# Batch 0's hi/lo parts stored to DRAM by halves of the heads, the first group's rows read between the two halves' stores

## The reference

```python
qkv = x @ w_qkv
q, k, v = jnp.split(qkv, 3, axis=2)                    # each (8, 512, 128) -> (8, 16, 512, 8)
att = jnp.einsum('bhtd,bhsd->bhts', q, k) / np.sqrt(D)
att = jnp.where(causal, att, -jnp.inf)
out = jnp.einsum('bhts,bhsd->bhtd', softmax(att), v)
x = layernorm(x + out.transpose(0, 2, 1, 3).reshape(B, T, C))
gate, up = x @ (w_gate/127).T, x @ (w_up/127).T
x = layernorm(x + (silu(gate) * up) @ (w_down/127).T)
```

## Time and profile before

| | us |
|---|---|
| three runs | 361.03, 364.29, 364.29 (median 364.29) |
| the profiled execution | 362.71 |
| its span, first to last instruction | 361.0 |
| TensorE busy | 338.2 (94%) |
| VectorE busy | 291.8 (81%) |
| ScalarE busy | 214.6 (59%) |
| GpSimd busy | 180.2 (50%) |

### The profile page before, as it was taken

One profiled execution on the slowest core, in us unless ns is written; L12 is line 12 of the kernel. 1 busy time (PEld: TensorE's weight loads), 2 busy tenths in 40 slices (PEclk: granted clock), 3 DMA queues, 4 the chain that ended last, 5 costly groups with the idle time before them and its releaser, 6 DMA issues.

```text
span 361.0 us, 9029 instructions
## 1 busy us (share of the span) xinstructions
PE 338.2 (94%) x2907; PEld 198.4 (55%) x2911; DVE 291.8 (81%) x1247; ACT 214.6 (59%) x277; POOL 180.2 (50%) x329
## 2 busy tenths in 40 slices
PE   4878999999999999999999999999999998999971
PEld 2533445556455645655564556556445544898961
DVE  6875658898888888988988898899898884868653
ACT  2400447877777677777867676876677774434310
POOL 8400133653384455447335734653433578787552
PEclk9996559999999999999999999999999969999997
DMA  4798330276337426532661553166200010011111
GB/s 145 279 301 246 83 86 5 63 254 190 91 126 229 120 63 236 155 112 86 228 190 37 188 170 120 33 237 202 66 4 5 5 30 3 1 36 53 46 44 58
DMA packets 33902, 41.73 MB, mean 116 GB/s; under 512 B 3136, under 2 KB 17472, under 8 KB 33856
## 3 DMA queue, kind: packets, MB, share of 16 engines
q1 hardware_dynamic: 33856, 41.17, 36.0%
HBM read 21.76 MB, written 18.87 MB: 113 GB/s over the span
## 4 chain that ended last, share of the span: by engine, by line
PE 79%; DVE 9%; issue 5%; DMA 3%; ACT 2%; POOL 1%; SPq 0%; DVEq 0%; POOLq 0%; ACTq 0%
PE psum L500 21%; PE psum L477 18%; PE psum L460 14%; PE psum L681 5%; DVE masked L853 5%; PE psum L416 5%; PE psum L407 4%; PE psum L669 3%; PE psum L671 3%; PE psum L442 2%; PE psum L509 2%; PE psum L432 2%; DMA scr_k<-parts 1%; DVE nm L853 1%; DMA xa<-L_attn_x 1%
## 5 line engine op out<-in xcount | busy, mean ns | idle before, releaser
L853 DVE CUSTOM_DVE_ANT_0 masked<-psum,mask 128x384 bf16<-128x384 f32 (+3 forms) x512 | 219.2, 487 | 37.5 <-PE psum L477 30.6
L756 ACT ACTIVATE pt<-psum 128x1024 f32<-128x1024 f32 x160 | 158.4, 1021 | 59.7 <-PE psum L460 59.2
L1028 POOL TENSOR_SCALAR_AFFINE_SELECT pt<-pt 128x512 f32<-128x512 f32 x128 | 79.7, 635 | 101.5 <-ACT pt L756 99.5
L477 PE MATMUL psum<-kx,qx 33*128 33x384 f32 (+3 forms) x512 | 93.5, 366 | 3.3 <-DMA kx<-scr_k 1.8
L500 PE MATMUL psum<-pt,vx 128*32 128x256 f32 (+2 forms) x1280 | 94.8, 397 | 0.1
L460 PE MATMUL psum<-qx,kx 35*128 35x384 f32 (+3 forms) x512 | 77.7, 353 | 0.9 <-DMA qx<-nm_T 0.8
L477 PEld LDWEIGHTS psum<-kx,qx 33*128 33x128 f32 x512 | 54.3, 193 | 40.9 <-DVE nm L853 19.1
L460 PEld LDWEIGHTS psum<-qx,kx 35*128 35x128 f32 x512 | 47.2, 192 | 30.4 <-issue 16.1
L500 PEld LDWEIGHTS psum<-pt,vx 128*32 128x32 f32 x1280 | 30.7, 110 | 39.0 <-issue 26.0
L853 DVE DVE_READ_ACCUMULATOR2_ANT nm<- 128x1 f32 x512 | 42.5, 83 | 0.0
L1016 POOL TENSOR_SCALAR nm_parts<-nm 128x16 fp32r<-128x16 f32 x32 | 6.6, 207 | 51.4 <-DVE nm L853 50.3
(11 more groups left out here) (64 smaller groups left out, 268.6 us busy)
## 6 DMA issues: line engine op xcount, KB each, us to landing
scr_q<-parts SPq DMA_DIRECT2D x16, 512.0 KB, 3.7
scr_k<-parts SPq DMA_DIRECT2D x16, 512.0 KB, 5.5
qx<-scr_q SPq DMA_DIRECT2D x64, 128.0 KB, 2.6
kx<-scr_k SPq DMA_DIRECT2D x64, 128.0 KB, 2.7
xa<-L_attn_x SPq DMA_DIRECT2D x8, 256.0 KB, 3.3
res<-L_attn_x SPq DMA_DIRECT2D x8, 256.0 KB, 2.8
out<-yo SPq DMA_DIRECT2D x8, 256.0 KB, 2.3
qx<-nm_T SPq DMA_DIRECT2D x64, 8.0 KB
```

The source lines that it names most:

```text
L477: last = pe.matmul(bank[:, col:col + width], qx[u][at:at + KM, 2 * g + hh // 2, P * i:P * i + P].bitcast(F32R), kx[u][at:at + KM, 2 * g + ...
L756: act.activation(pt[G % 2][:, 2 * s:2 * s + 2, :], pair_of("S", G, s), ACT.Exp, scale=SM_SCALE).then_inc(exp_done, 1)
L853: dve.tensor_tensor_reduce(masked[count % 4][:, 0:width], bank[:, col:col + width], mask[:, T - width:T], -1.0, 3.0e38, ALU.add, ALU.min, ...
L1028: pool.affine_select(out=blocks, in_=blocks, pattern=[[0, HG], [1, P]], compare_op=ALU.is_ge, fill=0.0, base=0, channel_multiplier=-1).the ...
```

## The change

Only batch 0 is touched. `write_half(half)` stores the 64 partitions of one half of the heads, again four DMAs, now of 256 KB each, with a semaphore of its own for each half. SP issues the first half's four stores, reads group 0's rows, issues the second half's four stores, and then reads the rows of groups 1, 2 and 3. A read of batch 0 waits for its own half alone. The later batches' stores are as they were, and their waits count from one batch less. `parts_of_1` on VectorE waits for both halves.

```diff
+        scr_half = [sem(f"scr_half{half}") for half in range(2)]
...
+            def write_half(half):
+
+                at = slice(64 * half, 64 * half + 64)
+                for n, scr in enumerate((scr_q[0], scr_k[0])):
+                    for part, made in enumerate((hi_made, lo_made)):
+                        sp.wait_ge(made, n + 1)
+                        terms = (scr[at, 2 * part:2 * part + 2, :], scr[at, part::2, :])[n]
+                        sp.dma_start(terms, parts[at, n, part, :].unsqueeze(1).to_broadcast([64, 2, T])).then_inc(scr_half[half], 16)
+
             def read_rows(b, u, g):
                 half, par = g // 2, g % 2
-                sp.wait_ge(scr_written, SCR * b + SCR)
+                if b == 0:
+                    sp.wait_ge(scr_half[half], SCR)
+                else:
+                    sp.wait_ge(scr_written, SCR * b)
...
-            write_parts(0, 0)
+            write_half(0)
             sp.wait_ge(rows_set, 2)
-            for g in range(NG):
+            read_rows(0, 0, 0)
+            write_half(1)
+            for g in range(1, NG):
                 read_rows(0, 0, g)
...
                     if n == 0:
-                        dve.wait_ge(scr_written, SCR)
+                        for half in range(2):
+                            dve.wait_ge(scr_half[half], SCR)
...
                     if n == 0:
-                        pool.wait_ge(scr_written, SCR * b)
+                        pool.wait_ge(scr_written, SCR * (b - 1))
```

## The result

The changed kernel took 372.0 us (median of six runs, 369.67 to 378.07) against 364.29 us: the ratio to the kernel before is 1.0218, 95% interval 1.0165 to 1.0272. The profiled execution took 373.35 us with a span of 371.6 us, 10.6 us more than before in both. The recorded forecast was 367.0 us, 369.2 us at the upper end: slower was right, the size was not.

The account below looks back on a forecast made before the run. Bound by the start's waits, VectorE's reductions, then TensorE. Early rows unused (0), VectorE late +1.35, clock +3.5, its return -0.6: +4.3 us on 362.71 gives 367.0 us, range 362.6 to 369.2.

Parts of the forecast that it names:

- What bounds the start: First 30 us: waits on stores and rows, then VectorE's reductions, then TensorE; both engines have some 1.8 us of slack.
- the half store's price: First half's stores: 0.69 us of data each at 381 GB/s, no queue, last landing at 13.2, 2.15 us earlier.
- the 1.77 us for TensorE: Group 0's rows land at 17.0, so TensorE's first maxima move from 19.52 to 17.75; not used on the path.
- the predicted timetable: Start of batch 0: first half 13.2, first maxima 17.75, second half 19.2, first reduction 21.5, 1.35 us late.
- The clock's term: TensorE in group 0: a 3.0 us idle stretch makes the clock fall at 22 to 23, costing 3.5 us.
- the prediction's own steps: Group 0 at half clock: each pair of banks with three dummies takes 2.1 us, from bank 3 at 22.15.
- the return of the clock: End of the half clock: same place of the program within one 2.1 us step, taken as -0.6 us.
- A fall of the clock at the old place: Clock falls at about 29 or a step later, leaving only VectorE's +1.35 us: 364.1 us; chance 0.22.
- early stores: Second half's stores land by 18.1, clock stays, reductions start at 20.3, change costs nothing: 362.8 us; chance 0.06.
- a shorter low stretch: Half-clock stretch from 28.96 to 52.80 runs at full clock: 356.3 us, 361.5 with a third saved; chance 0.07.
- The slower one: Second half lands at 20.3 among group 1's reads (+1.15), clock returns one step later (+1.5): 369.7 us; chance 0.10.
- SP behind it: SP's later issues: groups 2 and 3 out at 22.9 against 22.83, so batch 1's stores and all after cost nothing.

Follow-up runs that it names:

- the filled kernel: Changed kernel with 7 more dummies behind the first 8, 30 more at bank 3, 6 more before the first turn; ratio 1.0063.

## Why the prediction was wrong, step by step

**What bounds the start** held. The 1.8 us of slack on each engine, VectorE as the one that waits for the second half, the reductions behind it, and a loss that goes through to the end almost unchanged (10.47 us at the turn, 10.61 at the start of the last product with `w_down`) are all in the trace.

**The step that failed is the half store's price.** The prediction took 0.69 us of data for 262 KB "at that rate", the 381 GB/s of a store from all 128 partitions, concluded that "no queue forms", and held the store against the output store of 256 KB (2.3 us), which also leaves from 128 partitions. Neither row has anything to say of 64 adjacent ones. The rate was 211 GB/s, which is 1.24 us of data for each half store. That is more than the 0.7 to 1.0 us between their issues, so a queue did form: the four need 5.0 us of data, from 10 to 15 us in the windows. The last one took 4.41 us, outside the bounds of 2.0 and 2.8. The profile before had no such store, but it had transfers of few partitions: the reads, 32 partitions each and two places at a time, at 264 GB/s with a DMA share of 1.01, where the stores had 381. The row was used as the rate of reads; it was a warning that full DMA engines do not mean a full rate. The place of the Trainium skill that was weighed (DMA: Bandwidth & Descriptors, "Rules for kernel authors": one half serialises with the other) was not the one that mattered. The limit of 218 GB/s in the Trainium skill (SBUF — State Buffer, "Door 1: The DMA port swizzle") gives, as an estimate, 1.2 us of data for a half store where 0.69 was taken.

**What followed from it.** First half landed at 15.51 for 13.2, so the rows came no earlier and the 1.77 us for TensorE were never on offer. Second half landed at 24.90 for 19.2 (bounds 18.1 and 20.3), so the first reduction was 7.02 us late for 1.35. The four instructions of batch 1's parts took 2.13 us for 2.21. With the rate mended, the kernel on alternate partitions kept the predicted timetable to within 0.9 us up to the first reduction.

**The clock's term** had the right mechanism and was 0.7 us too small. The clock fell at about 22.3 ("22 to 23"), but the place was partly luck: in the changed kernel again it fell at about 19.6, already behind the first idle stretch. The prediction's 3.5 us reach to banks 2 and 3 of group 1, at 29.02 before. The change was there at 40.28, 11.26 us late, of which 7.02 are VectorE's; the clock's part is 4.2 us. The same stretch in the kernel on alternate partitions gives the same: banks 2 and 3 at 35.40, 6.38 us late, 2.14 of it VectorE's and 4.2 the clock's. From the first reduction to the turn alone it was 11.43 us against 7.98 at full clock, 3.45 more, where the prediction's own steps have 2.6. The difference lies in the first step (bank 3 and its dummies took 2.19 us and not 1.75) and ahead of the turn. That the turn of the filled kernel, at full clock, came 3.6 to 3.8 us earlier supports the cause. At the end the change was 10.61 us late, so the rest of the kernel, the return of the clock included, gave back 0.65 us for 0.6. The sum with measured terms is 7.02 + 4.24 - 0.65 = 10.61 us, against 10.64 between the profiled executions: 5.7 of the missing 6.4 us are the half store's price, 0.7 the clock's term.

**The rivals.** A fall of the clock at the old place, early stores, and a shorter low stretch all did not come: idle time was longer, stores later, and the low stretch 41 us and not 24. Where the clock falls is a matter of the single execution too, as the falls above show. The slower one, second half at 20.3, had the right place and sign, but its size was bounded by the same wrong rate. That SP behind it costs nothing held only in part: batch 1's stores were issued from 28.56 on and not from 22.87, and the first negated maxima's load waited for their copy behind TensorE's turn, not for them; in the kernel with own tiles batch 1's stores went out as late, from 28.20 on, and it cost nothing.

## What to carry to other kernels

A transfer's price has a third side beside bytes and count: which partitions it touches. Take its rate from a row of the same partition shape, and where none exists, put a bound of half the rate on a half tile of adjacent partitions (211 against 381 GB/s here). With that rate, compare a transfer's time with the spacing of the issues before calling a queue empty. If only half the rows are wanted early, laying them on every second partition keeps the rate; by itself that still lost 0.9% here. And before a store is put later, look for who overwrites its source: a tile of its own for the next writer took the whole 2.2% away, while the new order without it never gained.

## What the runs showed of the hardware

- A store from every second of 128 partitions moved its bytes at the rate of a full one: eight such stores landed 2.5 us (median) after their issue, against 4.1 to 4.6 us for eight from adjacent partitions, which includes their time in the queue. The first rows are of the kernel on alternate partitions, the others of the one with the halves first, DMA issues between 8 and 20 us (tensor, count, KB each, us to landing):

```profile
scr_q<-parts SPq DMA_DIRECT2D x4, 256.0 KB, 2.5
scr_k<-parts SPq DMA_DIRECT2D x4, 256.0 KB, 2.5
```

```profile
scr_q<-parts SPq DMA_DIRECT2D x4, 256.0 KB, 4.1
scr_k<-parts SPq DMA_DIRECT2D x4, 256.0 KB, 4.6
```

- What a store costs SP to issue differs from place to place, and these runs don't put it down to one thing. The first two `scr_q` stores took 0.37 us each with 128 partitions and 512 KB, and took 1.09 us for the pair both there and with 128 partitions and 256 KB; with 64 partitions, adjacent or alternate, the pair took 1.34 us. For `scr_k` it was the other way, 1.47 us for the pair before and 1.25 on alternate partitions. Where the stores of 128 partitions and 256 KB stand back to back, a pair took 1.16 to 1.34 us. The four issues of the change's second half took 3.6 us of SP where 2.3 were counted.
- The place and the length of the clock's low stretch vary, also between executions of nearly the same program. It lasted from 28.96 to 52.80 before, from about 20.0 to 23.4, with two more low stretches before 51, in the kernel before with own tiles, from 22.3 to 63.3 after and from 19.6 to 64.0 in the change again. One thing goes with it: in the four traces with 2.5 to 2.7 us of idle time ahead of the first maxima (own tile, its control, the gap at bank 3 filled, the change again) it fell between 19.0 and 20.0, and in the two with 1.58 and 1.78 us (after, before) it did not fall there. Why TensorE's dummies end about a us earlier in some executions was not followed. In the three kernels whose gaps were filled or closed no fall came before 37 us (about 37.8, 37.7 and 45.3), and in the eleven others it came between 19.0 and 29.0. TensorE was busy while the clock stayed low, 23.50 of 23.84 us before and 33.05 of the 35 us from 28 to 63 after. What ends the stretch was not tested.
